# A test-time-training scan beside cross-attention: the scan's first two products ahead of a step's scores, the second strip's scores behind the third product, slope ahead of the route's norm, mask rows in four strips

## The reference

```python
# L0 attn: a scan over the 16 batches (one step a batch); the state (W1, b1, W2, b2) takes one gradient step each
z, y, q = xn @ t_k.T, xn @ t_v.T, xn @ t_q.T
grads   = grad of mean((z + gelu(z @ W1.T + b1) @ W2.T + b2 - y)**2)
params  = params - 0.001 * grads
out     = q + gelu(q @ W1.T + b1) @ W2.T + b2          # with the new params
# L0 xattn: 16 heads of 8, 77 context tokens, a mask on the keys (all ones here)
s    = where(mask, q_h @ k_h.T / sqrt(8), -inf);  x += softmax(s) @ v_h @ Wo.T + bo
# L0 ffn: 8 experts of 512, top 2 by a router
# L1 attn: 16 heads over the batch's own 128 tokens, with a distance bias
# L1 xattn: as above, with s -= 10000 * (1 - mask);  L1 ffn: 8 experts, top 2
```

## Time and profile before

| | |
|---|---|
| median of three runs | 736.67 us |
| the profiled execution | 737.5 us, span 735.4 us |
| mean granted TensorE clock | 0.887 |
| PE busy / DVE / ACT / POOL | 79% / 66% / 58% / 49% |
| the scan's first product (round 0) | 64.81 us |
| the last (round 15) | 210.37 us |
| x1's scores | 502.06 to 595 us |

### The profile page before, as it was taken

The page is one execution under the profiler, slowest core; times in us unless marked ns, Lnnn a source line. Parts: engine busy times, 40 slices in busy tenths (PEclk is TensorE's granted clock), DMA queues, the critical chain, the costliest instruction groups (busy, mean ns, idle before and its releaser), DMA issues.

```text
span 735.4 us, 18464 instructions
## 1 busy us (share of the span) xinstructions
PE 581.9 (79%) x6145; PEld 464.0 (63%) x6160; DVE 484.9 (66%) x1361; ACT 428.3 (58%) x897; POOL 359.3 (49%) x646
## 2 busy tenths in 40 slices
PE   2896999998997617999469999987998961599970
PEld 1475767676765407999436767755676651599970
DVE  7643468778777443555348999884998975255536
ACT  1452268776775324888236676764685652387850
POOL 5711424555588672666443343322445857265550
PEclk9797579999999757999859999999999996699995
DMA  7779920000000012222370000000000001222215
GB/s 197 241 275 325 331 103 1 2 2 2 9 15 24 23 47 59 74 70 63 102 297 2 2 3 2 2 2 2 2 3 17 24 22 48 58 68 70 69 35 170
DMA packets 41706, 52.63 MB, mean 72 GB/s; under 512 B 10814, under 2 KB 36750, under 8 KB 41326
## 3 DMA queue, kind: packets, MB, share of 16 engines
q1 hardware_dynamic: 37069, 42.11, 18.2%
q0 software_dynamic: 4544, 9.35, 3.8%
HBM read 41.04 MB, written 28.22 MB: 94 GB/s over the span
## 4 chain that ended last, share of the span: by engine, by line
issue 69%; PE 11%; POOL 6%; SPq 2%; DVE 2%; DMA 1%; POOLq 0%; DVEq 0%
PE p_s L1672 5%; POOL yo L1578 5%; PE p_o L1682 3%; PE p_in L1682 2%; DVE x L1629 2%; POOL to_row L1573 1%; PE p_pT L1664 1%; SPq L1712 1%; SPq L288 1%; DMA yo<-context,to_row 1%; DMA context<-xs 0%; DMA back<-yo 0%; SPq L1697 0%; SPq L1701 0%; DVE context L1612 0%
## 5 line engine op out<-in xcount | busy, mean ns | idle before, releaser
L1578 POOL DMA_INDIRECT yo<-context,to_row x78 | 76.1, 976 | 69.0 <-DVE context L1612 36.6
L1636 ACT ACTIVATE context<-pack 128x1156 f32 x78 | 90.6, 1166 | 31.6 <-DVE context L1612 14.2
L1672 PE MATMUL p_s<-xT_f,context 128*128 128x128 f32 x624 | 85.9, 283 | 0.0
L1672 PEld LDWEIGHTS p_s<-xT_f,context 128*128 128x128 f32 x624 | 79.3, 199 | 0.0
L1122 POOL DMA_INDIRECT xs<-send,x_index x64 | 64.1, 1001 | 23.3 <-issue 17.0
L1605 DVE TENSOR_SCALAR context<-p_s,context 128x128 f32<-128x128 f32 x156 | 47.5, 346 | 29.0 <-PE p_s L1672 24.0
L1316 ACT ACTIVATE x_pT<-p_pT 128x512 f32<-128x512 f32 (+1 forms) x96 | 48.7, 525 | 20.7 <-PE p_pT L1418 18.2
L1643 ACT ACTIVATE context<-p_s,context 128x128 f32<-128x128 f32 x156 | 47.5, 357 | 21.6 <-PE p_s L1672 12.2
L1158 DVE TENSOR_REDUCE x_top<-p_s 128x12 f32<-128x924 f32 (+2 forms) x48 | 47.1, 1009 | 17.6 <-PE p_s L1404 17.2
L1418 PE MATMUL p_pT<-sq,x_prob 128*128 128x128 f32 x320 | 51.6, 285 | 5.7 <-ACT x_pT L1316 2.8
L1168 DVE TENSOR_TENSOR x_prob<-p_s,x_top 128x768 f32<-128x768 f32 (+2 forms) x96 | 50.0, 576 | 0.1
(11 more groups left out here) (255 smaller groups left out, 1493.8 us busy)
## 6 DMA issues: line engine op xcount, KB each, us to landing
xs<-in_blank SPq DMA_DIRECT2D x2, 8707.5 KB, 43.5
pack<-in_pack SPq DMA_DIRECT2D x16, 578.0 KB, 8.0
context<-xs SPq DMA_DIRECT2D x78, 64.5 KB
back<-yo SPq DMA_DIRECT2D x16, 256.0 KB, 4.5
yo<-context,to_row POOLq DMA_INDIRECT x78
x<-in_x SPq DMA_DIRECT2D x4, 256.0 KB, 4.3
xs<-send,x_index POOLq DMA_INDIRECT x64
out<-x SPq DMA_DIRECT2D x4, 256.0 KB, 2.3
```

The costliest lines, as they stand in the source:

```text
L1578: nc.gpsimd.indirect_dma_start(yo[:, :], bass.IndirectOffsetOnAxis(to_row[:, n % NY, :], 0), y[:, n % NY, :], None).then_inc(y_stored[n % ...
L1636: nc.scalar.activation(ws[:, n % NW, :], pack[:, bass.ds(e, 1), :].rearrange("p a w -> p (a w)"), ACT.Copy).then_inc(ws_ready, 1)
L1672: ins = mm(p_h[n % 2][k // 2][:, P * (k % 2):P * (k % 2 + 1)], ws[:, n % NW, P * k:P * (k + 1)], xT[:, n % 2, :], start=True, stop=True)
```

## The change

- TensorE's list: `aT` and `aq` stand ahead of `score`; `score` now does the masks and strips 0, 2 and 3, then comes `a`, and then a new entry `score_rest` with the wait for `strips_scored` and strip 1. `rturn` moves from between `e_` and `dh` to between `g1` and `mix`.
- VectorE's list: `w1n` ahead of `count`, `rcount` behind `w2Tn`.
- ScalarE's list: `c_rturn` moves from behind `e` to behind `c_q`, next to `exp`.
- GpSimd's list: `slope1` ahead of `rnorm`.
- The mask rows are written at the start of all four strips (16 small DMAs on SP in place of 4), and a mask product has 1 or 3 rows of one strip in place of 128 rows.
- `project` waits for one `c_rturn` fewer, `rturn` waits for `c_q` in place of `c_turn`.

```diff
-FIRST_PE = ((3, "score"), (0, "aT"), (1, "aq"), (0, "a"), (4, "tp0"), (5, "po"), (0, "eT"), (2, "turn_in"), (1, "gw2"), (4, "tp1"), (1,
-    "out"), (0, "e_"), (7, "rturn"), (0, "dh"), (4, "tp2"), (8, "rank"), (2, "project"), (0, "g2"), (0, "g1"), (4, "mix"), (0, "g1b"), (7,
+FIRST_PE = ((0, "aT"), (1, "aq"), (3, "score"), (0, "a"), (3, "score_rest"), (4, "tp0"), (5, "po"), (0, "eT"), (2, "turn_in"), (1, "gw2"), (4, "tp1"), (1,
+    "out"), (0, "e_"), (0, "dh"), (4, "tp2"), (8, "rank"), (2, "project"), (0, "g2"), (0, "g1"), (7, "rturn"), (4, "mix"), (0, "g1b"), (7,
     "rlogit"))
 FIRST_DVE = ((5, "scale"), (8, "choose"), (3, "max"), (0, "eTa"), (5, "res"), (1, "w2n"), (0, "slope2"), (0, "slope3"), (1, "comb"), (0,
-    "da"), (8, "address"), (3, "shift"), (1, "count"), (0, "w1n"), (5, "rcount"), (0, "b1n"), (0, "w2Tn"))
-FIRST_ACT = ((0, "hT"), (1, "hq"), (0, "acopy"), (4, "pT0"), (2, "c_turn"), (0, "h"), (4, "pT1"), (0, "e"), (7, "c_rturn"), (4, "pT2"), (2,
-    "c_q"), (3, "exp"), (7, "c_rlg"))
-FIRST_POOL = ((2, "rstd"), (2, "norm"), (0, "slope0"), (7, "rnorm"), (0, "slope1"), (9, "scat"), (2, "kT"), (6, "rrstd"))
+    "da"), (8, "address"), (3, "shift"), (0, "w1n"), (1, "count"), (0, "b1n"), (0, "w2Tn"), (5, "rcount"))
+FIRST_ACT = ((0, "hT"), (1, "hq"), (0, "acopy"), (4, "pT0"), (2, "c_turn"), (0, "h"), (4, "pT1"), (0, "e"), (4, "pT2"), (2, "c_q"), (7,
+    "c_rturn"), (3, "exp"), (7, "c_rlg"))
+FIRST_POOL = ((2, "rstd"), (2, "norm"), (0, "slope0"), (0, "slope1"), (7, "rnorm"), (9, "scat"), (2, "kT"), (6, "rrstd"))
...
-                        sp.dma_start(m["mask_0"][0:1, :, :].rearrange("a b k -> a (b k)"), mk_0[:, :]).then_inc(m["masks_placed"], 16)
-                        for r in range(3):
-                            sp.dma_start(m["mask_1"][r:r + 1, :, :].rearrange("a b k -> a (b k)"), mk_1[:, r, :]).then_inc(m["masks_placed"], 16)
+                        for g in range(NG):
+                            r0 = STRIP * g
+                            sp.dma_start(m["mask_0"][r0:r0 + 1, :, :].rearrange("a b k -> a (b k)"), mk_0[:, :]).then_inc(m["masks_placed"], 16)
+                            for r in range(3):
+                                sp.dma_start(m["mask_1"][r0 + r:r0 + r + 1, :, :].rearrange("a b k -> a (b k)"),
+                                             mk_1[:, r, :]).then_inc(m["masks_placed"], 16)
...
-        banks = (range(0, 6), range(6, 12), range(12, 16))
+        banks = ((range(0, 6), 0), (range(6, 12), 2), (range(12, 16), 3))
...
             if q is not None:
-                wait(pe, xr_sb, FIRST + b - LAG + 1)
+                wait(pe, xr_sb, FIRST + b - LAG + (0 if beside else 1))
...
-            for bank, hs in enumerate(banks):
+            for bank, (hs, strip) in enumerate(banks):
                 to = p_s[:, bank, 0:len(hs) * T]
                 if mask:
-                    mm(to.rearrange("p (h k) -> p h k", k=T), rows_on,
-                       m[mask][:, b, :].unsqueeze(1).to_broadcast([P, len(hs), T]), start=True, stop=False)
+                    r = slice(STRIP * strip, STRIP * strip + mask_rows)
+                    mm(to.rearrange("p (h k) -> p h k", k=T), ones_bf[r, :],
+                       m[mask][r, b, :].unsqueeze(1).to_broadcast([mask_rows, len(hs), T]), start=True, stop=False)
...
-            for g in (0, 2, 3, 1) if beside else range(NG):
+            score_strips(b, p, (0, 2, 3) if beside else range(NG))
+
+        def score_strips(b, p, order):
+            for g in order:
...
+        def score_rest(b, p):
+
+            pe.wait_ge(strips_scored, 2 * (b + 1))
+            score_strips(b, p, (1,))
...
             if beside:
-                pe.wait_ge(turned_sb, min(b + LAG + 1, NB))
+                pe.wait_ge(q_sb, min(b + LAG + 1, NB))
```

More of the change, by code:

```diff
@@ L296, in _ @@
                 pool.wait_ge(m["scan_sems"]["set_up"], 2)
-                pool.wait_ge(m["masks_placed"], 64)
+                pool.wait_ge(m["masks_placed"], 64 * NG)
                 nc.gpsimd.memset(m["x_work"]["prob"][:, :, NH * KM:], 0.0).then_inc(m["x_sems"]["set_up"], 1)
@@ L979, in attention @@
     p_s, p_pT, p_in, p_o = m["p_s"], m["p_pT"], m["p_in"], m["p_o"]
-    if mask:
-        rows_on = (m["ident_bf"][:, 0:1] if mask_rows == 1 else m["before"][:, mask_rows:mask_rows + 1]).to_broadcast([P, P])
     if beside:
@@ L992, in attention @@
         heads = [(0, NH, HG, p_s[:, :, 0:GW].rearrange("p g (h k) -> p g h k", k=T))]
-        banks = [range(HG * g, HG * (g + 1)) for g in range(NG)]
+        banks = [(range(HG * g, HG * (g + 1)), g) for g in range(NG)]
         strips = [[(0, HG, g, 0)] for g in range(NG)]
@@ L1387, in score @@
             if FIRST + b == 0 and mask:
-                pe.wait_ge(m["masks_placed"], 64)
-            for bank, hs in enumerate(banks):
+                pe.wait_ge(m["masks_placed"], 64 * NG)
+            for bank, (hs, strip) in enumerate(banks):
                 to = p_s[:, bank, 0:len(hs) * T]
                 if mask:
-                    mm(to.rearrange("p (h k) -> p h k", k=T), rows_on,
-                       m[mask][:, b, :].unsqueeze(1).to_broadcast([P, len(hs), T]), start=True, stop=False)
+                    r = slice(STRIP * strip, STRIP * strip + mask_rows)
+                    mm(to.rearrange("p (h k) -> p h k", k=T), ones_bf[r, :],
+                       m[mask][r, b, :].unsqueeze(1).to_broadcast([mask_rows, len(hs), T]), start=True, stop=False)
                 else:
@@ L1397, in score @@
             pe.wait_ge(k_sb, FIRST + b + 1)
-            for g in (0, 2, 3, 1) if beside else range(NG):
+            score_strips(b, p, (0, 2, 3) if beside else range(NG))
+        def score_strips(b, p, order):
+            for g in order:
                 r = slice(STRIP * g, STRIP * (g + 1))
-                if beside and g == 1:
-                    pe.wait_ge(strips_scored, 2 * (b + 1))
                 for i0, i1, bank, at in strips[g]:
@@ L1407, in score @@
                     last.then_inc(strips_scored, 1)
-            last.then_inc(scored, 1)
+            if not beside or g == 1:
+                last.then_inc(scored, 1)
+        def score_rest(b, p):
+            pe.wait_ge(strips_scored, 2 * (b + 1))
+            score_strips(b, p, (1,))
         def turn_p(groups):
@@ L1499, in tensor @@
         if beside:
-            return dict(score=score, turn_in=turn_in, project=project, tp0=turn_p((0,)), tp1=turn_p((1,)), tp2=turn_p((2,)), mix=mix, po=project_o,
+            return dict(score=score, turn_in=turn_in, project=project, tp0=turn_p((0,)), tp1=turn_p((1,)), tp2=turn_p((2,)), mix=mix, score_rest=score_rest, po=project_o,
                         rturn=route_turn, rlogit=logits, rank=rank)
```

## The result

The changed kernel takes 741.34 us (median of 6 runs, 741.2 to 743.18) against 735.45 for the kernel before (6 runs, 733.67 to 737.41): a ratio of 1.0085, with an interval of 1.0061 to 1.011. It is slower by 0.85%. The forecast was 732.3 in a range of 724 to 740: the time went the other way, and lies outside the range. The profiled execution took 741.39 us, its span is 739.3. Four executions in the experiments lie far off the others (763, 1115, 1850 and 1852 us); they are in the medians, not in the ratios.

What follows compares the result with a forecast made beforehand. TensorE's chain bounded rounds without the router's part, VectorE's wait for GpSimd those with it, VectorE x1. Second stage -2.4 and x1 -2.0 made -4.4: 737.5 to 733.1, the median 0.8 lower, 732.3 us; range 724 to 740.

Steps and rivals of the forecast that it cites:

- the sum for the second stage: Slices 4 to 14: gains in rounds 3 to 7, 17 and 18, 0 in 8 to 15, +1.1 in 16; together -2.4 us.
- Round with router's part, 10.07: Second stage, rounds 8 to 15: 10.07 us, or 10.18 by a second chain, against 10.09; table load hides slope's gain.
- load not displaced: Rival, ScalarE's Exp table load: not delayed by c_rturn, so aq goes at about 2.7, round 9.06, kernel 724; chance 0.14.
- Round without it, 8.54: Second stage, a round without the router's part, from g1 to the next g1: 8.54 us against 8.88.
- `a` between the strips: TensorE's list, second stage: a fills about 0.1 us of idle time; two more tiling mode changes cost 0.15 together.
- That wait ... its price is the whole difference: Rounds 7 to 15: VectorE's slope2 idles for GpSimd, with slope1 behind rnorm; 1.21 us, all that these rounds take longer.
- x1, 2.0 of at most 6.9: Stage x1: shorter masks save 0.43 us a step, mainly where VectorE waited for TensorE; 2.0 us taken, bounds 0 and 6.9.
- VectorE does: Stage x1: VectorE, busy 45.47 of 50 us, bounds the steps rather than TensorE; it waited for TensorE in 6 steps.
- Mask DMAs: Start of the kernel: twelve more at 0.62 us each end before GpSimd asks; nothing, up to 1 if the cover failed.
- VectorE's order: Second stage: w1n comes 0.46 us sooner but TensorE is busy until after it, scale moves some 0.1, hidden; nothing.
- `project`'s wait: Second stage: c_rturn of the same round is no longer ahead of project; 0.15 us, inside the 3.71 from tp0 to g1.
- The slower rival: Rounds 3 to 15: masks in turn +0.39, mode changes drain +0.3, so 0.69 by 13, 9.0, kernel 741 us; chance 0.11.

Runs made afterwards that it cites:

- `rturn` back: The changed kernel with rturn and c_rturn, and the waits that go with them, in their places of before: 725.93 us, ratio 0.9885 to the kernel before.
- `aq` later: The changed kernel with aq behind a and ahead of score_rest: 722.46 us, ratio 0.988 to the kernel before; once more on the third chip 720.02 us, 0.9871.
- 32-row masks: The changed kernel with mask products of 32 rows in each strip, the others zero, in place of 1 or 3: 734.03 us, ratio 1.006 to the kernel before.

## Why the prediction was wrong

**The step that failed** is the sum for the second stage: "Rounds 8 to 15: 0. ... Round 16 ... + 1.1 ... Rounds 17 and 18: masks, 0.4", that is +0.7 for rounds 8 to 18, all of it costed at 2.4 GHz. It measured +12.07 between the `max` of round 8 and that of round 18. The same text forecast "TensorE idle between `aT` and `aq` by 1.2 us" and masks in a third of their time, and began with a clock "granted in full from slice 6 on" (the page has 7 tenths in slice 6 and 9 from slice 7 on, and 3.4 us at 1.2 GHz in slice 11); it never asked whether the clock would stay so in the new order. It didn't: from round 8 to round 18 the changed kernel ran 38.7 us at 1.2 GHz, the kernel before 3.4. With products in place of the wait the same stretch takes 103.71, +2.0, with 11.8 us at 1.2 GHz still in it. So about 10 of the 12 us are the clock, by the stretches that these products removed. End to end that kernel is at 0.999 of before.

**Round with router's part, 10.07**: 9.87 and 10.03 in the two full rounds of the profile that have no stretch at 1.2 GHz; right within 0.2, and right in its pieces (`exp` +2.18, `aq` +3.71). The rival "load not displaced" (9.06 a round, 724 us) took 1.0 a round for the wait. With the load back at its place (`rturn` back) a round is 9.38, 0.49 less. With the load late and the wait filled with scores (`aq` later) it is 8.85, 1.02 less. Their ratios are 0.9885, and 0.988 and 0.9871: some 727 us by the median of before beside the change.

**Round without it, 8.54**: 8.17. Masks alone bring 0.54 (8.88 to 8.34), where 0.39 was taken, and `a` between the strips another 0.17, where +0.05 net was taken. Two changes of tiling mode more a round cost nothing that can be seen. The Trainium skill, "TensorEngine Tiling (Array Packing)", Key Properties, says that such a change drains TensorE; by that this edit should lose, and the rows don't bear it out. Rounds 3 to 7 gained 3.27 where 3.1 was forecast.

**"That wait ... its price is the whole difference"** (`slope2` behind `rnorm`, 1.21): wrong. Slope first alone leaves rounds at 10.1, since `rturn` is held by the same norm, and masks in strips alone take 0.45 from those rounds. They are one loop through TensorE and GpSimd: `g1`, masks, strips, `a`, `slope0`, the norm, `dh`, `da`. Time taken from any part that lies on it counts, and a wait at one place of it didn't say that the rest was free. That they are one loop is argued from these two runs and the lists, not tested by a run of its own. It did not decide the sign, as the changed order moves `rturn` too.

**x1, 2.0 of at most 6.9**: 3.0, all of layer 1's attention counted. "VectorE does" was too simple. In a step of before that no wait of the list disturbs, `max` still began 0.07 behind the end of the strips, so a part of the mask's time stood in every such step; now it begins 1.24 behind it, VectorE alone sets the pace, and 0.20 of the 0.43 is gone (5.44 to 5.24). But there are only five such steps in a row. 2.1 us came from the step into x1 and the first one, where TensorE held `max` (12.97 to 12.38, and 7.19 to 5.72, which has a stretch at 1.2 GHz in both kernels).

**Mask DMAs, VectorE's order, `project`'s wait**: nothing to be seen, as forecast. The slower rival named the masks in turn and mode switches for its 741; its time was met by luck, since the masks run side by side and the switches cost nothing that can be seen.

**Open**: what in the work brings the clock down. Busy time of 9.91 in 10 us went with both outcomes, 9.20 with the full clock, 8.95 (after, 142.5 to 152.5) with a fall at 152.8. The wait for `c_rlg` went with both as well. Strips in place of whole masks, together with a changed order, is what the falls before round 12 have in common; which property of the strips it is was not separated. That the 32-row masks change little speaks against the number of rows within a strip.

## What to carry to other kernels

- Where a forecast takes work from TensorE in a loop that runs at 2.4 GHz with little slack, give a fall of the clock a chance and a price of its own: here masks shorter by 0.3 us, in a round of 10 that also had 1.0 us of wait, went with a loss of some 10 us over ten rounds, more than the edits could bring. The wait by itself did not do it.
- Run the parts of a change one by one: strips alone took 1.1% off, and the four lists changed with them put 2% on.
- A copy that is put ahead of the first Exp holds back its table load; before it is moved, see what stands behind the Exp and who shares its bank. Moving the waiter behind other ready work (`aq` behind the scores) was worth 2%.
- A wait for an engine is the price of that step only if nothing else waits for the same producer; look for every reader of it.

## What the hardware showed that was not expected

- Three one-row mask products in three strips take 0.37 to 0.38 us against 0.69 to 0.71 for three whole ones, and the next strips can begin 0.15 behind them.
- More work made the kernel faster: with five unused products a round its ratio to before is 0.999 instead of 1.0085.
- A kernel at 99% busy TensorE (9.91 of 10 us) was put at 1.2 GHz for 3.4 us at 159.1, and another with the same busy time was not. A third, whose TensorE waited 0.96 us a round, kept 2.4 GHz from 102.9 to 232.6.
